# Attention and mixture of experts on one core: the first slot's stacks in two loads, another order of the steps, and row maxima that run over the turn's end

## The reference

```python
qkv = x @ W_qkv                      # x: 16 x 1024 x 256
q, k = rope(q), rope(k)              # rotation by halves of each head
att = q @ k.T / 4 + causal_mask      # 1024 x 1024 for each of 16 heads
y = softmax(att) @ v
x = layernorm(x + y @ W_o)
gate = softmax(x @ Wg + bg)          # the two largest, divided by their sum
out = sum over experts of gate * (x @ We[e].T + be[e])
x = layernorm(x + out)
```

## Time and profile before

| | us |
|---|---|
| median of 3 runs | 3246.15 (3246.06 to 3248.67) |
| profiled execution, as timed | 3247.9 |
| its span, first to last instruction | 3246.2 |
| TensorE busy | 3110.3 (96%) |
| VectorE busy | 2684.6 (83%) |
| ScalarE busy | 1885.3 (58%) |
| GpSimd busy | 1198.2 (37%) |

### The profile page before, as it was taken

How to read it: one execution, slowest core, us unless ns; L and a number is a source line. 1 busy time by engine, 2 the same in 40 slices (tenths; PEclk the granted TensorE clock), 3 DMA queues, 4 the chain that set the end, 5 groups by cost and what they waited for, 6 DMA issues and landing times.

```text
span 3246.2 us, 58552 instructions
## 1 busy us (share of the span) xinstructions
PE 3110.3 (96%) x18752; PEld 1712.3 (53%) x18752; DVE 2684.6 (83%) x8456; ACT 1885.3 (58%) x4257; POOL 1198.2 (37%) x1410
## 2 busy tenths in 40 slices
PE   4789999999999999999999999999999999999987
PEld 2234555555555555555555555555555555555555
DVE  6877888888888888888988888888888888888745
ACT  2266556575565656556575665657565565755551
POOL 3153424444243443424344342434324344442110
PEclk8699999999999999999999999999999999999997
DMA  5344324333442434334333442443443243344000
GB/s 134 62 70 81 60 57 77 62 68 66 80 65 50 78 58 79 60 76 65 55 73 61 83 65 57 73 66 68 66 83 60 55 79 61 69 65 70 4 27 14
DMA packets 174819, 210.95 MB, mean 65 GB/s; under 512 B 26008, under 2 KB 124592, under 8 KB 174256
## 3 DMA queue, kind: packets, MB, share of 16 engines
q1 hardware_dynamic: 173056, 202.98, 35.9%
q10 hardware_dynamic: 1456, 4.23, 0.3%
HBM read 138.44 MB, written 67.11 MB: 63 GB/s over the span
## 4 chain that ended last, share of the span: by engine, by line
PE 84%; DVE 8%; issue 3%; ACT 2%; POOL 1%; DMA 1%; ACTq 0%; SPq 0%; DVEq 0%; POOLq 0%
PE bank L917 22%; PE attend L1012 15%; PE scores L990 14%; PE bank L974 14%; PE bank L954 6%; PE bank L1036 3%; PE bank L963 3%; DVE bank L775 2%; PE bank L1020 1%; PE bank L942 1%; DVE maxima L778 1%; PE bank L1027 1%; PE bank L1044 1%; ACT weights L651 1%; PE bank L1068 1%
## 5 line engine op out<-in xcount | busy, mean ns | idle before, releaser
L651 ACT ACTIVATE weights<-scores 128x512 f32<-128x512 f32 (+3 forms) x3072 | 1333.5, 495 | 886.0 <-PE scores L990 872.7
L775 DVE CUSTOM_DVE_ANT_0 bank<-bank,far_q 128x128 f32<-128x128 f32 (+3 forms) x2048 | 963.1, 512 | 202.7 <-PE bank L974 187.2
L974 PE MATMUL bank<-k_stack,q_stack 96*128 96x512 bf16 (+3 forms) x3072 | 803.6, 333 | 31.7 <-DVE maxima L775 10.5
L990 PE MATMUL scores<-q_stack,k_stack 99*128 99x512 bf16 (+3 forms) x3072 | 821.1, 328 | 10.6 <-ACT weights L651 6.9
L571 POOL TENSOR_SCALAR_AFFINE_SELECT weights<-weights 128x512 f32<-128x512 f32 x512 | 325.4, 637 | 1269.4 <-ACT weights L651 1269.1
L778 DVE TENSOR_REDUCE maxima<-bank 128x1 f32<-128x512 f32 x1024 | 643.9, 682 | 71.2 <-PE bank L974 70.9
L1012 PE MATMUL attend<-weights,values 128*32 128x512 f32 (+3 forms) x6144 | 579.2, 492 | 1.0 <-POOL weights L571 0.9
L990 PEld LDWEIGHTS scores<-q_stack,k_stack 99*128 99x128 bf16 x3072 | 280.1, 97 | 411.8 <-ACT weights L651 154.6
L974 PEld LDWEIGHTS bank<-k_stack,q_stack 96*128 96x128 bf16 x3072 | 276.9, 98 | 400.6 <-issue 153.6
L917 PE MATMUL bank<-wexp_hi,zT_hi 128*128 128x512 f32 x1024 | 381.7, 454 | 11.1 <-DVE lowrows L795 11.1
L891 DVE SCALAR_TENSOR_TENSOR z<-bank,picked,z 128x256 f32<-128x256 f32 x512 | 247.5, 483 | 113.8 <-PE bank L917 104.9
(11 more groups left out here) (110 smaller groups left out, 3133.5 us busy)
## 6 DMA issues: line engine op xcount, KB each, us to landing
parts_scratch<-parts SPq DMA_DIRECT2D x128, 384.0 KB, 2.5
q_stack<-parts_scratch SPq DMA_DIRECT2D x384, 128.0 KB, 7.1
k_stack<-parts_scratch SPq DMA_DIRECT2D x384, 128.0 KB, 7.7
x_in<-in_x SPq DMA_DIRECT2D x64, 256.0 KB, 3.6
z<-in_x SPq DMA_DIRECT2D x32, 512.0 KB, 5.3
out<-z SPq DMA_DIRECT2D x32, 512.0 KB, 3.2
q_stack<-lowrows SPq DMA_DIRECT2D x192, 8.0 KB, 2.4
z<-in_w_exp ACTq DMA_DIRECT2D x1, 1024.0 KB, 4.9
```

The lines of the kernel that those rows point to most:

```text
L651: act.activation(weights[:, n % NW, hh, c0:CH], st[(QUAD * n + hh) % NS][:, c0:CH], ACT.Exp, scale=DH ** -0.5).then_inc(S["weights_ready"], 1)
L775: dve.tensor_tensor_reduce(out=b[:, 0:w], in0=b[:, 0:w], in1=far_q[:, CH - w:CH], scale=1.0, scalar=-SENTINEL, op0=ALU.add, op1=ALU.max, a ...
L974: pe.matmul(b[:, 0:w], q_stack[0:ROWS, n, hh, qt * P:(qt + 1) * P], k_stack[0:ROWS, n, hh, kc * CH:kc * CH + w], start=True, stop=True).th ...
L990: pe.matmul(st[(QUAD * n + hh) % NS][:, c0:CH], k_stack[0:MROWS, s, hh, kb * P:(kb + 1) * P], q_stack[0:MROWS, s, hh, qc * CH + c0:(qc + 1 ...
```

## The change

It has four parts.

- **Row maxima later.** The items 4 to 11 of slot 1 (`LATE_B = 4`; eight items of four heads, so 32 `B`) leave the stretch ahead of their batch and are done in the batch's own turn, as `B.3.4.0` and on. `pre` has 16 `B` of slot 1 instead of 48, and no `MC.1` and `MT.1`; `last` has 32 `B` more.
- **Another table.** Within a turn every other step has a new place too. Two of them matter further on: `MT.2`, the transposed maxima of the next batch's slot 0, stood behind `ST.38.3` and stands behind `ST.47.0`; and `GLT.0 GA.0 GB.0 GT.0`, the gates of the first half of the tokens, are closer together.
- **The first eight heads on DVE.** In `pre`, the first four halves are rotated by DVE alone, which reads PSUM directly (no copy by ACT) and does all four operations and both subtractions. The other four are rotated and subtracted by POOL alone, as in the turns.
- **Two loads.** In `pre`, slot 0's stacks come in two parts: tokens 0 to 511 by a step `EARLY`, the rest by `LOAD.0`. The expert weights are split between the two groups of heads, and slot 0's `B` start before the last half is rotated.

The diff, cut to these. The new functions and the order of `pre`:

```diff
+LATE_B = 4
-    if step in (("MC", SLOTS - 1), ("MT", SLOTS - 1)):
-        return seg in ("mid", "last")
+    if step in (("MC", SLOTS - 1), ("MT", SLOTS - 1)) or (kind == "B" and s == SLOTS - 1 and step[2] >= LATE_B):
+        return attend
...
+        cast = [("CAST", *half, n) for half in halves[:4] for n in range(2)]
+        out += [("QK", *halves[0]), ("ROPE", *halves[0]), ("QK", *halves[1]), ("ROPE", *halves[1]), cast[0]]
+        out += [("QK", *halves[2]), ("ROPE", *halves[2]), cast[1], cast[2]]
+        out += [("QK", *halves[3]), ("ROPE", *halves[3]), cast[3], ("EARLY",), cast[4], ("QK", *halves[4]), ("ROPE", *halves[4])]
+        out += [cast[5], cast[6], cast[7], ("LOAD", 0), ("WSPLIT",)]
+        cast = [("CAST", *half, n) for half in halves[4:] for n in range(2)]
+        out += [*cast[0:2], ("QK", *halves[5]), ("ROPE", *halves[5]), ("VP", 0), ("VP", 1), *cast[2:4], ("LOAD", 1)]
+        out += [("QK", *halves[6]), ("ROPE", *halves[6]), ("VP", 2), ("VP", 3), ("QK", *halves[7])]
+        out += scores[:8] + cast[4:6] + [("ROPE", *halves[7])] + scores[8:16] + cast[6:8] + [("LOAD", 2)] + scores[16:]
+        out += [("MC", 0), ("MT", 0)]
+        out += [("B", 1, it, hh) for it in range(LATE_B) for hh in range(QUAD)]
...
+def on_vector(seg, step):
+    return seg == "pre" and step[1] == 0
...
+                elif kind == "EARLY":
+                    wait_all(*((f"parts_stored{i}", c.at(f"parts_stored{i}", ("CAST", 0, i, 1), DMA)) for i in range(2)))
+                    for t, parts_qk in enumerate(TERMS):
+                        for which, stack in enumerate((q_stack, k_stack)):
+                            src = scratch[which, parts_qk[which], 0:QUAD, :, 0:CH]
+                            sp.dma_start(stack[DH * t:DH * (t + 1), 0, :, 0:CH], src.rearrange("h d t -> d h t")) \
+                              .then_inc(S["early"], DMA)
...
+                elif kind == "ROPE" and on_vector(c.seg, step):
+                    dve.stream_shuffle(rope_swap[:, :], bk[n][:, :], SWAP).then_inc(S["swapped"], 1)
+                    dve.tensor_tensor(x1, bk[n][:, :], cos[:, ch * CH:(ch + 1) * CH], ALU.mult).then_inc(free[n], 1)
...
+                    dve.tensor_tensor(rope_swap[:, :], rope_swap[:, :], sin[:, ch * CH:(ch + 1) * CH], ALU.mult) \
+                       .then_inc(S["sines"], 1)
...
+                    dve.tensor_tensor(x1, x1, rope_swap[:, :], ALU.add).then_inc(S["rotated"], 1)
```

Of the table, the last line of a turn:

```diff
-ST.47.0 B.3.10.2 B.3.10.3 B.3.11.0 VP.2 B.3.11.1 ST.47.1 B.3.11.2 VP.3 ST.47.2 ST.47.3 MASK.47 B.3.11.3
+ST.47.0 MT.2 VP.2 B.3.2.3 B.3.3.0 B.3.3.1 ST.47.1 ST.47.2 ST.47.3 MASK.47 VP.3 B.3.3.2 B.3.3.3
```

More of the change, by code:

```diff
@@ new lines @@
+ST.29.0 ST.29.1 GLT.1 ST.29.2 B.1.9.3 ST.29.3 B.1.10.0 B.1.10.1 B.1.10.2
+ST.30.0 ST.30.1 B.1.10.3 ST.30.2 B.1.11.0 ST.30.3 GA.1 PV.28 CAST.1.2.0 PV.29
+ST.31.0 ST.31.1 ST.31.2 QK.1.3 GB.1 B.1.11.1 ST.31.3
+ST.32.0 B.1.11.2 B.1.11.3 ST.32.1 GT.1 B.2.0.0 ST.32.2 ST.32.3 CAST.1.2.1 B.2.0.1 MC.1 MASK.32 PV.30 ROPE.1.3
+  B.2.0.2 B.2.0.3 B.2.1.0 B.2.1.1 PV.31 B.2.1.2 R2.0
+ST.33.0 YT.2.0 BE.1.0 BE.1.1 MOE.1.0.0 MOE.1.0.1 ST.33.1 B.2.1.3 B.2.2.0 MOE.1.0.2 ST.33.2 B.2.2.1 MOE.1.0.3
+  MOE.1.1.0 ST.33.3 MASK.33 B.2.2.2 MT.1
@@ L266, in ledger @@
                 add(f"parts_stored{step[2] % 2}", seg, step)
-            if step[0] == "ROPE":
+            if step[0] == "ROPE" and not on_vector(seg, step):
                 add("turning", seg, step)
-                if seg == "pre":
-                    add("sines", seg, step)
-    return book
+            if step[0] == "ROPE" and on_vector(seg, step):
+                add("sines", seg, step)
+    return book
+def on_vector(seg, step):
+    return seg == "pre" and step[1] == 0
 def stack_of(seg, step):
@@ L452, in run, with half_of @@
                         work(c, turn + 1, "END")
+        def half_of(c, s, k):
+            return weights[:, 0, k] if on_vector(c.seg, ("ROPE", s, k)) else rope[:, k % 2]
         def rest(eng, c, s, k, n):
-            x1 = rope[:, k % 2]
+            x1 = half_of(c, s, k)
             eng.wait_ge(S["cast"], c.at("cast", ("CAST", s, k, n)))
@@ L497, in work @@
                     n = stack_of(c.seg, step)
+                    first = CH if c.seg == "pre" and s == 0 else 0
                     if c.seg != "pre" and s == 0:
@@ L572, in work @@
                                        pattern=[[0, QUAD], [1, P]], channel_multiplier=-1).then_inc(S["masked"], 1)
-                elif kind == "CAST" and (c.seg != "pre" or a[2]):
+                elif kind == "CAST" and not on_vector(c.seg, step):
+                    if c.seg == "pre" and a[1] == 0:
+                        name = ("rest_ready", "parts_ready")[a[2]]
+                        pool.wait_ge(S[name], c.below(name, step, 1))
+                        pool.sem_inc(S["pool_waits"], 1)
                     rest(pool, c, *a)
@@ L609, in work @@
                                    ACT.Copy).then_inc(fr, 1)
+                elif kind == "QK" and on_vector(c.seg, step):
+                    return
                 elif kind == "QK":
@@ L780, in work @@
                     (s,) = a
-                    emptied(dve, c, ("B", s, ITEMS - 1, QUAD - 1), prev=s == SLOTS - 1 and c.seg != "pre")
+                    emptied(dve, c, ("B", s, ITEMS - 1, QUAD - 1))
                     m = maxima[:, s % 2].rearrange("p (h t) -> p h t", h=QUAD)[:, :, 4:TILES]
@@ L802, in work @@
                     dve.stream_shuffle(rope_swap[:, :], rope[:, k % 2], SWAP).then_inc(S["swapped"], 1)
-                    if c.seg == "pre":
-                        dve.wait_ge(S["swapped"], c.at("swapped", step))
-                        dve.tensor_tensor(rope_swap[:, :], rope_swap[:, :], sin[:, k // 2 * CH:(k // 2 + 1) * CH], ALU.mult) \
-                           .then_inc(S["sines"], 1)
-                elif kind == "TURN":
-                    s, k = a
-                    dve.wait_ge(S["turning"], c.at("turning", ("ROPE", s, k)))
-                    hold()
-                    dve.wait_ge(S["sines"], c.at("sines", ("ROPE", s, k)))
-                    dve.tensor_tensor(rope[:, k % 2], rope[:, k % 2], rope_swap[:, :], ALU.add).then_inc(S["rotated"], 1)
-                elif kind == "CAST" and c.seg == "pre" and a[2] == 0:
+                elif kind == "CAST" and on_vector(c.seg, step):
                     rest(dve, c, *a)
@@ L970, in work @@
                     w = min(CH, P * (qt + 1) - CH * kc)
-                    if it == 0 and hh == 0:
+                    if c.seg == "pre" and s == 0:
+                        if it in (0, 4) and hh == 0:
+                            name = "early" if it == 0 else "stack0"
+                            pe.wait_ge(S[name], LOADS)
+                            pe.sem_inc(S["pe_waits"], 1)
+                    elif it == 0 and hh == 0:
                         pe.wait_ge(S[f"stack{n}"], c.so_far(f"stack{n}", step, LOADS))
```

168 lines of the change are left out of this document (80 added, 88 removed).

## The result

The changed kernel takes 3257.49 us (median of 6 executions, 3256.67 to 3259.17), the kernel before beside it 3246.34. The ratio is 1.003, with a 95% interval of 1.0018 to 1.0041: slower by 0.3%. A second comparison in the experiments gave 1.0023 (1.0014 to 1.0033). The forecast was 3256, and slower.

The account below looks back on a forecast made before the run. TensorE's queue was taken to bound the turns, the rotation's chains and VectorE's maxima the prologue. 3247.9 − 41 (prologue) + 43 (turns, 3.1 each) + 7.5 (`last`) = 3257.4, so a median of 3256; range 3230 to 3280.

Parts of the forecast that it names:

- The prologue, 41 us: Stretch ahead of `first`: `first` starts at about 97.5 instead of 138.37, 41 us gained, kept range 30 to 46.
- The halves: In `pre`: slot 0's `B` end 16.2 us earlier; slot 1's removed `B` and the input delay behind them save 23.5.
- Rival 4: In `pre`: sixth half waits for the weights' split, ports shared badly; 30 us won instead of 41, 3267, slower; chance 0.10.
- The ports: In `pre`: VectorE's split and POOL's fifth half queue for shared SBUF ports, putting the sum some 3 us higher.
- The input's wait: At `XT.0` in each turn: loads queue behind `MT.2`'s transfers, 7.3 us against 4.9 of work; net 2.1 us a turn.
- The lower price for the load: Input load before `XT.0`: a skill page's 2.6 us instead of 3.0, making the sum some 5 us lower.
- The gates: Between `GLT.0` and `GT.0` in each turn: a wait of 1.1 us, less 0.74 at the first `MOE`; net +0.4.
- The rest: Elsewhere in each turn: VectorE is full behind `QK.1.3`, 0.6 us of waits, bounds 0 and 1.4.
- `last`, +7.5: In `last`: 32 more `B` at 5.3 us, with waits for the gates and slot 0's maxima 7.5; bounds 5 and 11.
- Rival 1: At `XT.0` in the turns: input is there in time, turns cost 0.5 each, 3220, faster; chance 0.12.
- Rival 2: In the turns: only the input delay costs, 1.9 us each, 3240, at the edge of faster; chance 0.22.
- rival 3: In the turns: VectorE's clusters and POOL's blocked queue add 4.5 us a turn, 3276, slower; chance 0.15.

Follow-up runs that it names:

- the loads first: The changed kernel, with SP issuing the next batch's first two loads ahead of `MT.2`'s three transfers instead of behind them: 3218.79 us, ratio 0.9898.
- late `B` and table alone: The kernel before, with the changed kernel's table and 16 `B` of slot 1 in `pre`, its own rotation and single load kept: 3271.04 us, ratio 1.0065.

## Why the prediction was right, step by step

- **The prologue, 41 us: right, and nearly by its own steps.** `XT.0` at 96.97, forecast 97.5. The halves measured 16.8 and 23.5 against 16.2 and 23.5. (These two make 39.7; the last 1.2 us of the 41 were put down to the slack of the four banks, which no row of the prediction shows.) Inside, the fifth half's shuffle went at 37.2 (forecast 39.7), the sixth's at 52.6 (55), the last maximum of slot 0 ended at 87.4 (89.6). The sixth half's shuffle did not go behind the weights' split, as the forecast has it: VectorE was through at 51.3 and stood 1.26 us for ScalarE's copy, which stands behind the two casts that the early load's transfers had held up. So the early load won nothing, as said, but "costs nothing" was wrong: it held ScalarE up by 6.5 us and spared TensorE 7.4, and that the two cancel is luck. Rival 4 is out.
- **The ports.** A VectorE pass of 0.68 us took 1.58 beside POOL's:

```profile
39.76 1.26 POOL L577 TENSOR_TENSOR rope_swap<-rope_swap,sin_sb 128x512 f32<-128x512 f32 x1
41.10 1.59 POOL L580 TENSOR_TENSOR rope<-rope,rope_swap 128x512 f32<-128x512 f32 x1
...
39.99 1.58 DVE L465 TENSOR_TENSOR weights<-weights,parts 128x512 f32<-128x512 f32 x1 [1.31 <-ACT parts L647]
...
45.70 2.29 DVE L778 TENSOR_TENSOR wexp_lo<-z,wexp_hi 128x2048 fp32r<-128x2048 f32 x1
47.98 2.28 DVE L778 TENSOR_TENSOR wexp_lo<-heads,wexp_hi 128x2048 fp32r<-128x2048 f32 x1
49.43 1.85 POOL L465 TENSOR_TENSOR rope<-rope,parts 128x512 f32<-128x512 f32 x1 [6.74 <-ACT parts L647]
```

  The 3 us that were to come on top by the rule did not: the rotation of POOL's fifth half was through at 42.7, before the split's long subtractions began, and both of them took 2.3 us. Only the half's first subtraction met the second of them, and took 1.85 us where POOL's later ones take 1.15; 0.7 us, not 3. The Trainium skill, "SBUF — State Buffer", section "SBUF: two separate sides", which has the two engines hold the ports by turns, agrees with the pairs in these rows; the sum that I made by it placed the pair wrongly.
- **The input's wait: right in size, wrong in what it costs.** The chain from `MT.2` was to take 7.3 us and took 7.36; the wait was to be 2.4 and 0.2, less 0.5, and was 2.1 in all, less 0.5, so net 1.6 where 2.1 stood. The step that failed is the one after it, "ScalarE and VectorE run dry behind it and give nothing back": it counted the wait alone. The fall of the granted clock behind it costs another 1.55 us a turn (1.8 us of added busy time, of which 0.24 stay in the kernel with the loads first). The wait's price was 3.1 us, not 2.1. The lower price for the load did not hold here: from SP's issue at 1223.24 to `XT.0` at 1226.19 it is 2.95 us in the timeline of the result, near the 3.0 that the sum used. By the Trainium skill, "DMA: Bandwidth & Descriptors", section "Anatomy of one DMA — SWDGE (gpsimd) path", it would be 2.6, an estimate that only the shortest load of the trace reaches.
- **The gates: over-sized.** The wait at `GT.0` is 0.26 us, forecast 1.1, and `MOE.0.0.0`'s 0.74 are gone: net −0.5 where +0.4 stood. TensorE's work between the two was 4.3 as counted; VectorE needed 4.56 from one transpose to the other with a `B` of 0.69 inside, where the earlier trace rows give 4.21 without one. The timeline shows where the `B` lies:

```profile
1273.83 0.21 DVE L881 TENSOR_REDUCE logits<-bank 128x32 f32<-128x64 f32 x1
1273.97 0.69 DVE L800 TENSOR_REDUCE maxima<-bank 128x1 f32<-128x512 f32 x1
...
1274.58 0.29 DVE L888 MAX8 top<-logits 128x8 f32<-128x8 f32 x3
```

  and without a `B`, in the kernel before's `post`:

```profile
3204.68 0.22 DVE L851 TENSOR_REDUCE logits<-bank 128x32 f32<-128x64 f32 x1 [1.72 <-PE bank L1060]
3205.04 0.31 DVE L858 MAX8 top<-logits 128x8 f32<-128x8 f32 x3
```

  The `B` comes between the reduction of the logits and their largest values, which start 0.75 us apart here and 0.36 in the stretch of the earlier trace rows, where VectorE stands idle for 0.14 of them. So the `B` costs 0.4 and not 0.65. The two ahead of it cost nothing: from `GLT`'s start to the reduction it is 0.64 us here and 0.65 there.
- **The rest: over-sized.** 0.6 us a turn stood for VectorE's clusters. The kernel with the loads first has the same table, and besides the two waits named above (0.90 and 0.27) its turns show nothing but the 0.24 of busy time. The new order is as dense as the old one without paying for it.
- **The turn's sum.** 3.1 forecast, 2.60 measured: 1.6 for the wait, 1.55 for the clock, −0.5 for the gates, 0.24 of other busy time, and by difference −0.3, of which some 0.1 is that the windows hold 13 of the 14 waits, the rest being small waits of the old order that the new one has not. Two terms that were too large stood for one that was missing, and the total was right in part by that.
- **`last`, +7.5: measured +7.3, by other terms.** The forecast was 5.3 for the `B` and 2.2 for waits. The wait at `GT.0` is there, 2.4 us, but the idle time of `last` as a whole did not grow (7.05 us, 7.66 before). The `B` are 4.6 of busy time, by the version with the late `B` and table alone, whose `last` has the same steps at full clock (161.49 against 156.92). The other 3.3 are the clock again, which fell behind the wait at `GT.0`; where it didn't, `last` is 168.6 and not 171.8. That the number is right is luck.
- **`first`, 0 ± 6: measured +5.3.** 3.6 are idle time (17.5 us, 13.9 before), and of these 1.6 the input's longer wait at its end; 1.7 are busy time, the fall of the clock at 148.5 us. With the old table and the new prologue `first` took 154.2, with the new table and the old prologue 159.0, so it is the table.
- **`post`, 0: +1.3** in this execution. The profiled ones lie from 100.1 to 105.2 with the same matmuls, and TensorE's busy time in them from 70.1 to 75.4: the clock, and no step of the change.
- **The rivals.** Rival 1 (input in time) fell by 2 us of wait in every turn. It was right about the mechanism, though: with the input in time the kernel would win, and the loads first show by how much, 3213 for its 3220. Rival 2 asked for turns of 1.9 more, rival 3 for 4.5; 2.6 lies between rival 2 and the forecast.
